# Three chained dense products on 64 graphs beside an eigendecomposition: the hidden product in seven chained products, one masking operation for two, sums of weights over six steps

## What is computed

```python
def _slconv(x, adj, S, W):
    support = jnp.einsum('bnf,fh->bnh', x, W)
    weighting = adj * S
    return jnp.einsum('nm,bmh->bnh', weighting, support)
h = relu(_slconv(h, adj, S, W1))     # 256 -> 512 features: "hid"
h = relu(_slconv(h, adj, S, W2))     # 512 -> 1024
return _slconv(h, adj, S, W3)        # 1024 -> 256
# h at the start is relu(layernorm(x)); the result is added to x
...
# second layer: eigenvectors U of the normalised Laplacian of A = adj
_, U = jnp.linalg.eigh(L_norm)
agg = jnp.einsum('mn,bnd->bmd', U.T, features)
h = relu(agg @ W1 + b1)
out = h @ W2 + b2
return jnp.einsum('nm,bmd->bnd', U, out)
```

## Time and profile before

| what | value |
| --- | --- |
| median of three runs (lowest, highest) | 2261.66 us (2261.61, 2262.51) |
| the profiled execution: own time, span | 2262.78 us, 2261.1 us |
| TensorE busy (modelled ends) | 2238.3 us, 99% |
| VectorE busy | 1932.7 us, 85% |
| ScalarE busy | 1151.1 us, 51% |
| GpSimd busy | 1159.6 us, 51% |
| granted TensorE clock | 1.00 |
| DMA | 90.14 MB, mean 40 GB/s |

### The profile page before, as it was taken

How to read it: one execution, slowest core, us unless ns; L and a number is a source line. 1 busy time by engine, 2 the same in 40 slices (tenths; PEclk the granted TensorE clock), 3 DMA queues, 4 the chain that set the end, 5 groups by cost and what they waited for, 6 DMA issues and landing times.

```text
span 2261.1 us, 47549 instructions
## 1 busy us (share of the span) xinstructions
PE 2238.3 (99%) x12586; PEld 1905.3 (84%) x12586; DVE 1932.7 (85%) x10818; ACT 1151.1 (51%) x2901; POOL 1159.6 (51%) x1889
## 2 busy tenths in 40 slices
PE   8999999999999999999999999999999999999999
PEld 5777888888888888888888888888888888889998
DVE  7999999999888888888777778989999997547776
ACT  5555555555555555555555544444444444344554
POOL 6455555545555555555555557544555554343332
PEclk9999999999999999999999999999999999999999
DMA  3000000000000000000000000000000001024443
GB/s 105 29 29 29 16 24 29 29 29 20 29 29 29 29 29 19 19 28 28 28 28 28 28 29 20 29 29 19 24 25 28 28 28 38 19 80 132 135 132 107
DMA packets 90031, 90.14 MB, mean 40 GB/s; under 512 B 5376, under 2 KB 89088, under 8 KB 89856
## 3 DMA queue, kind: packets, MB, share of 16 engines
q1 hardware_dynamic: 89856, 88.23, 12.2%
HBM read 54.66 MB, written 33.55 MB: 39 GB/s over the span
## 4 chain that ended last, share of the span: by engine, by line
PE 91%; DVE 7%; ACT 1%; issue 1%; POOL 0%; DVEq 0%; ACTq 0%; POOLq 0%
PE ps L1550 74%; PE ps L1740 10%; PE ps L1472 3%; PE ps L1750 1%; DVE A L961 1%; PE ps L1683 1%; DVE A L965 1%; ACT squares L709 1%; DVE prods L998 1%; DVE xrow_sb L970 1%; ACT root_s L711 0%; DVE ps L1013 0%; DVE sc L979 0%; DVE sc L982 0%; DVE qcol L984 0%
## 5 line engine op out<-in xcount | busy, mean ns | idle before, releaser
L501 POOL COPY Eb<-sc 128x1 f32<-128x1 f32 (+1 forms) x254 | 46.7, 184 | 451.6 <-DVE v L986 231.9
L1550 PE MATMUL ps<-agg2T,w 128*128 128x256 f32 x1024 | 239.2, 379 | 0.0
L1550 PE MATMUL ps<-hid2T,xin 128*128 128x256 f32 x1024 | 236.1, 379 | 0.7 <-ACT h2T L754 0.7
L1550 PE MATMUL ps<-weightT,hid 128*128 128x256 f32 x1024 | 236.7, 379 | 0.0
L1550 PE MATMUL ps<-w,aggT 128*128 128x512 f32 x512 | 231.7, 592 | 0.0
L1550 PEld LDWEIGHTS ps<-weightT,hid 128*128 128x128 f32 x1024 | 189.5, 191 | 36.7 <-issue 14.3
L1550 PEld LDWEIGHTS ps<-hid2T,xin 128*128 128x128 f32 x1024 | 189.0, 190 | 26.2 <-ACT h2T L754 1.1
L1550 PEld LDWEIGHTS ps<-agg2T,w 128*128 128x128 f32 x1024 | 188.5, 190 | 25.3
L754 ACT ACTIVATE hid2T<-ps 128x512 f32<-128x512 f32 x256 | 151.0, 590 | 94.9 <-PE ps L1550 92.9
L1166 DVE SCALAR_TENSOR_TENSOR ahead<-ps,ne,ahead 128x14 f32<-128x14 f32 (+1 forms) x1020 | 189.9, 228 | 0.0
L1163 DVE RECIPROCAL ps<-ahead 128x14 f32<-128x14 f32 (+1 forms) x1024 | 188.3, 230 | 0.1
(11 more groups left out here) (387 smaller groups left out, 6194.3 us busy)
## 6 DMA issues: line engine op xcount, KB each, us to landing
xl<-in_x_dram SPq DMA_DIRECT2D x64, 256.0 KB, 2.8
xr<-in_x_dram SPq DMA_DIRECT2D x64, 256.0 KB, 2.8
x_dram<-xr SPq DMA_DIRECT2D x64, 256.0 KB, 2.3
xin<-x_dram SPq DMA_DIRECT2D x64, 256.0 KB, 2.8
out_dram<-xin SPq DMA_DIRECT2D x64, 256.0 KB, 2.2
w<-in_L_gnn_W_dram SPq DMA_DIRECT2D x1, 2048.0 KB, 10.3
w<-in_L_gnn_W_dram SPq DMA_DIRECT2D x1, 1024.0 KB, 12.2
w<-in_L_gnn_W_dram SPq DMA_DIRECT2D x1, 512.0 KB, 5.2
```

The lines of the kernel that those rows point to most:

```text
L501: pool.tensor_copy(Eb[:, bass.ds(k, 1)], sc[:, 4:5])
L1550: ins = pe.matmul(dst, a, b, start=start, stop=stop, skip_group_check=plan_.units[i][0][0] in "PG")
```

## The change

1. **hid.** The four units of `hid` (each two matmuls of 512 columns) become seven, `H1 H5 H6 H2 H7 H3 H4`, each two matmuls of 256 columns. As in P and G, H6 adds onto H1's bank, H3 onto H5's, H7 onto H6's and H4 onto H7's, after the bank was evacuated. GpSimd makes four sums of nodes for each pair (`sum_of_nodes`, into the tile h) and three additions of results (`add_hid`); ScalarE makes seven evacuations and three relus (`finish_hid`) in place of four evacuations. The banks of the units are no longer taken in turn but by the table `bank_of`.
2. **Steps of two blocks.** The two instructions of L1013 become one (`tensor_tensor` with `under`, a copy of the mask in PSUM), and the clearing of L1015 goes; `columns` leaves the head out of the squares instead.
3. **Sums of weights.** Four sums of W1 are made before the first step; those of W2 and W3, made in steps 0 to 3 of pair 0, are made in steps 1 to 5, in another order, and the P units wait for each by itself.
4. `COUNTS_AT`, `REFLECTORS_AT`, `REFINE_AT`, `TURN_AT`, `VECTORS_AT` and `NORMS_AT` are set anew for a pair of 43 units instead of 40.

```diff
         def columns(k0):
 
-            return max(k0, P) if k0 + 1 >= P else k0
+            return max(k0, P) if k0 + 1 >= P else k0 + 1
...
-        COUNTS_AT, REFLECTORS_AT = 34, 3
-        REFINE_AT, TURN_AT, VECTORS_AT = (24, 27, 34, 38, 41, 43, 46), 63, 65
-        NORMS_AT = 22
+        COUNTS_AT, REFLECTORS_AT = 39, 7
+        REFINE_AT, TURN_AT, VECTORS_AT = (38, 41, 48, 50, 53, 55, 59), 75, 77
+        NORMS_AT = 33
...
-            units = [("hid", j, q) for j in range(2) for q in range(NB)]
+            units = [(p, 0, 0) for p in ("H1", "H5", "H6", "H2", "H7", "H3", "H4")]
...
+        BANK_OF = {"H1": 0, "H5": 1, "H6": 0, "H2": 2, "H7": 0, "H3": 1, "H4": 0, "agg": 2, "res": 2}
+        BANK_OF.update({p + n: 0 if n in "1674" else 2 for p in "PG" for n in "1567324"})
+
+        def bank_of(unit):
+            stage, j, q = unit
+            return (3, 2, 0, 1)[2 * q + j] if stage == "agg2" else BANK_OF[stage] + j
...
-        S_TURNS = [(n, half) for half in range(2) for n in (1, 2, 3, 4)]
+        S_TURNS = [(n, half) for n in (1, 2, 4, 3) for half in range(2)]
...
+        HID_ADDS = (("C11", "H1", "H2"), ("C12", "H6", "H3"), ("C22", "H5", "H7"))
...
-        POOL_ORDER = [("turn", n) for n in range(1, 5)] + [("add", n) for n in range(len(ADDS))]
-        POOL_ORDER += [("left", n) for n in range(len(LEFTS))] + [("g3", n) for n in range(len(G3_ADDS))]
+        POOL_ORDER = [("hid", n) for n in range(3)] + [("turn", n) for n in range(1, 5)] + [("add", n) for n in range(len(ADDS))]
+        POOL_ORDER += [("left", n) for n in range(len(LEFTS))] + [("nodes", n) for n in range(1, 5)] + [("g3", n) for n in range(len(G3_ADDS))]
...
+            def sum_of_nodes(pair, n):
+
+                a11, a12, a21, a22 = (aggT[:, j, f, :] for j in range(2) for f in range(2))
+                a, b, op = {1: (a21, a22, ALU.add), 2: (node_block(1), a11, ALU.subtract), 3: (a11, a21, ALU.subtract),
+                            4: (a12, node_block(2), ALU.subtract)}[n]
...
+                pool.tensor_tensor(node_block(n), a, b, op).then_inc(node_sum, 1)
+
+            def add_hid(pair, n):
+
+                name, other, block_ = HID_ADDS[n]
+                pool.wait_ge(evac, before(pair) + FULL.at[block_, 0, 0] + 3)
+                pool.tensor_tensor(hid_block(name), hid_kept(other), hid_block(name), ALU.add).then_inc(hid_added, 1)
...
                     if isinstance(t, int) and t == 0:
                         if s == 0:
+                            pool.wait_ge(evac, 4)
+                            for n in range(1, 5):
+                                sum_of_nodes(0, n)
+                        if s == 1:
                             pool.wait_ge(load_w, 16 * 6)
-                        for n, half in S_TURNS[4 * s:4 * s + 4]:
+                        for n, half in S_TURNS[3 * (s - 1):3 * s] if s else []:
                             sum_of_weights(n, half)
-                        if 2 <= s < 4:
+                        if 4 <= s < 6:
...
+            def finish_hid(pair, n):
+
+                act.wait_ge(hid_added, len(HID_ADDS) * pair + n + 1)
+                block_ = hid_block(HID_ADDS[n][0])
+                act.activation(block_, block_, ACT.Relu).then_inc(hid_fin, 1)
...
+            HID_AFTER = {5: [0], 6: [1], 7: [2]}
...
                 dve.wait_ge(col_ready, k + 2)
-                for b in range(NB):
-                    ins = dve.tensor_scalar(x_next[:, b:b + 1], col[:, b:b + 1], below[:, b, here:here + 1], None, ALU.mult)
-                at(ins)
-                at(dve.memset(head, 0.0), HOUSE - 20)
+                at(dve.tensor_tensor(x_next, col[:, :], under[:, :, here], ALU.mult), HOUSE - 19)
...
-                if stage == "hid":
-                    return group(bank[:, :], [(aggT[:, j, f, P * q:P * q + P], w1[:, f, :]) for f in range(FB)])
+                if stage[0] == "H":
+                    left, right = {"H1": (aggT[:, 0, 0, :], w1_block(0, 0)), "H2": (aggT[:, 0, 1, :], w1_block(1, 0)),
+                                   "H3": (node_block(4), w1_block(1, 1)), "H4": (aggT[:, 1, 1, :], w1sum[:, 3, :]),
+                                   "H5": (node_block(1), w1sum[:, 0, :]), "H6": (node_block(2), w1sum[:, 1, :]),
+                                   "H7": (node_block(3), w1sum[:, 2, :])}[stage]
+                    return [(half[m], left[:, P * m:P * m + P], right, "P" + stage[1] not in ONTO and m == 0, True)
+                            for m in range(NB)]
...
+                if (stage, j, q) == ("agg2", 1, 0):
+                    pe.wait_ge(evac, before(pair) + plan_.at["H4", 0, 0] + 3)
+                elif stage == "agg2":
+                    pe.wait_ge(hid_fin, len(HID_ADDS) * pair + (1, 1, 2, 3)[2 * q + j])
```

More of the change, by code:

```diff
@@ L349, in needs @@
                 return [("add", n)]
+            if kind == "hid":
+                return [("evac", at[HID_ADDS[n][2], 0, 0])]
+            if kind == "hidfin":
+                return [("hid", n)]
+            if kind == "nodes":
+                return [("evac", at["agg", 1, 0])]
             if kind == "turn":
@@ L380, in placed @@
                     if events and all(x in ended for x in needs(*events[0])):
-                        engine = "act" if line in ("evac", "fin") else line
+                        engine = "act" if line in ("evac", "fin", "hidfin") else line
                         start = max([free[engine]] + [ended[x] + 0.1 for x in needs(*events[0])])
-                        ready.append((start, line != "fin", line, engine))
+                        ready.append((start, line not in ("fin", "hidfin"), line, engine))
                 start, _, line, engine = min(ready)
                 kind, n = event = lines[line].pop(0)
-                took = {"unit": size[n] * 62.0 / total if kind == "unit" else 0, "g3": 0.75, "fin": 0.65,
+                took = {"unit": size[n] * 62.0 / total if kind == "unit" else 0, "g3": 0.75, "nodes": 0.75, "fin": 0.65, "hidfin": 0.65,
                         "evac": 0.35 if kind == "evac" and FULL.units[n][0][0] == "G" else 0.65}.get(kind, 1.35)
@@ L410, in placed @@
             return early, late, pool_turns
-        for first, last, steps, _ in GROUPS:
-            assert last - first == 1 or steps % 2 == 0
+        for (first, last, steps, _), k0 in zip(GROUPS, FIRST_STEP):
+            assert last - first == 1 or steps % 2 == 0 and k0 + 1 >= P
         @block.sync
@@ L592, in in_turn @@
                     sum_of_moving(pair, n)
+                elif kind == "hid":
+                    add_hid(pair, n)
+                elif kind == "nodes":
+                    sum_of_nodes(pair + 1, n)
                 elif kind == "add":
@@ L664, in pair_sums @@
             def pair_sums(pair, more, plan_=FULL):
+                for n in range(3):
+                    add_hid(pair, n)
                 for n in range(1, 5):
@@ L672, in pair_sums @@
                         ln_scale(pair + 1, j)
-                for kind, n in POOL_ORDER[4:]:
-                    in_turn(pair, kind, n, plan_)
+                for kind, n in POOL_ORDER[7:]:
+                    if kind != "nodes" or more:
+                        in_turn(pair, kind, n, plan_)
             with pool.Fori(WITH_STEPS, PAIRS - 1) as t:
@@ L753, in evacuate @@
                     act.wait_ge(turn_s, 4 * pair + 4)
-                act.activation(dst, bank, ACT.Relu if stage in ("hid", "P4") else ACT.Copy).then_inc(evac, 1)
+                act.activation(dst, bank, ACT.Relu if stage in ("H4", "P4") else ACT.Copy).then_inc(evac, 1)
             def finish(pair, n):
@@ L846, in pair_body @@
                         finish(pair, n)
+                    for n in HID_AFTER.get(i, []):
+                        finish_hid(pair, n)
                     if more and (stage, j) == ("P2", 1):
@@ L1483, in unit_matmuls @@
                 stage, j, q = plan_.units[i]
-                bank = ring[i % 4]
+                bank = ring[bank_of(plan_.units[i])]
                 half = [bank[:, 0:N], bank[:, N:2 * N]]
```

77 lines of the change are left out of this document (57 added, 20 removed).

## The result

The changed kernel took 2293.28 us (median of 4 runs, 2292.82 to 2293.94), the kernel before beside it 2261.89 (2261.61 to 2262.51): ratio 1.0139, 95% interval 1.0121 to 1.0156. That is 31.4 us slower. The forecast was 12 us slower, with 2284 as the upper end of its range: the sign was right, the size was not.

A forecast was written before the change was run, and what follows sets the result against it. TensorE's own sum was taken to bound most of the kernel, VectorE the start. Terms 5.3 + 4.8 + 2.0 + 0 = +12.1 us on the 2261.1 span, plus 0.6, gave 2273.8 us; range 2265 to 2283, with rivals 2256 to 2284.

The forecast's parts named there:

- Pairs 22 to 31, no steps: Pairs after the reduction: waits of 0.8 us a pair against a gain of 0.84, so no change over ten pairs.
- The last two pairs ... 0: Last two pairs: eigenvector places and a 1.47 us wait for VectorE move; gain may be taken back, counted as 0.
- The weights' sums ... nothing: Early steps: weights' sums of 1.27 us each on GpSimd, at most three a step, used three steps later, cost nothing.
- Rival (c): GpSimd becomes late, step 1's reflector copy passing the next beta and stopping VectorE: 2286 us, chance 0.08.
- a gain of 0.84 for the products: Every pair: hid's matmul passes on TensorE fall from 6.88 to 6.04 us, a gain of 0.84 us.
- the waits of two-block steps: Pairs 5 to 11: TensorE waits 0.33 in step 0, 1.2 in the next; less 0.84, +0.7 us a pair, +4.8 in all.
- Pairs 1 to 3: Pairs where VectorE sets the pace: delays in steps 0 and 1 outweigh VectorE's gain, net +0.5 us a pair.
- the two delays of 0.9 and 1.76: VectorE-paced pairs: q row 0.9 us late in step 0 and 1.76 us late in the next step.
- 1.6 and 0.36: VectorE-paced pairs: 0.18 us saved per step by the single instruction, 1.6 over nine steps and 0.36 over steps 0 and 1.
- Pairs 12 to 20: One-block pairs, forecast as 12 to 21: waits of 0.10 and 1.0, later steps gain 0.86; +0.1 to +0.25 a pair, +2.0.
- 1.6 too little in pair 0: Pair 0: GpSimd's first sums of nodes come behind step 0's reflector copies, delaying TensorE; taken as 3 us in all.
- Rival (a): Throughout the kernel: the forecast waits are absent through unseen slack, 30 us less, 2232 us, chance 0.10.

The follow-up runs named there:

- the run with only the halves moved: Changed kernel with only GpSimd's halves (masks of zeros and ones for the reflector products) moved to pairs 2 to 8: 2289.74 us, ratio 1.0119.

## Why the prediction was wrong in size

The step that failed is the paragraph "Pairs 22 to 31, no steps", with its "nothing is left, 0 x 10". Its working holds for the pairs behind pair 22. Pairs 25 to 28, beside which TensorE does nothing else, took 57.36 us each before and 57.47 after (from the first `weightT,hid` pass to the next pair's), and pairs 23 to 29 together are 0.1 us longer: the three handovers and the relu cost about what the seven products gave. It took pair 22 for one of them. I read the GpSimd rows of a later pair, found 4.61 us of idle time, and never read GpSimd's list at the seam (the place where the steps end and the pairs without steps begin), though the earlier trace rows is itself a view of 1399 to 1401.5 us. The change moved GpSimd's first duty in a pair from behind `agg2` to behind H2, and 17.7 us of other work stood in between. That is 12.3 + 1.8 of the 19 us by which the forecast was short, shown by taking the block away (14.1 by the medians, 13.7 between two passes of the traces).

The same oversight in small is in three other terms. "The last two pairs ... 0" missed that GpSimd's list has the second layer's scalars ahead of pair 31's additions (3.0 us). "The weights' sums ... nothing" missed that those of W3 come between the additions of pair 0 (step 6: 8.52 us for 5.99). And the W1 sums before the first step, which I left out of the sum altogether, held VectorE by 1.9 in the changed kernel's trace. Rival (c) was the right suspect, a late GpSimd, at the wrong place: it looked at reflector copies, which were never late.

What held: a gain of 0.84 for the products (steps 5, 8 and 10 of pair 8 are 0.43, 0.23 and 0.22 shorter), and the waits of two-block steps: of the 1.5 us forecast, step 1 of pair 8 is 1.23 longer and step 0 0.21, and the pair is longer by 0.57 (forecast 0.7). Putting the relu ahead of the root gave back 0.8 of it, so the cause of that wait is shown. Pairs 1 to 3 were 0.3 shorter rather than 0.5 longer. Both halves of that term were off. The run without VectorE's part is 2.0 us a pair above the kernel before there, where the forecast had 2.46 (the two delays of 0.9 and 1.76, less 0.2 for the lighter last steps); and VectorE's part took off 2.3 beside the products, where I had 1.96 (1.6 and 0.36). Pairs 12 to 20 were longer by 0.46 each rather than 0.1 to 0.25. Up to pair 21 the loss was 13.9 us against 12.1 in my terms, and that closeness is in part luck: 3.0 too much in pairs 1 to 4 and 0.8 too much in pairs 5 to 11 hid 1.6 too little in pair 0, 2.2 too little in pairs 12 to 20 and the 1.8 at the start. Rival (a), no waits, is out; with the waits taken away by order and banks the kernel comes to 2237.6, near that rival's 2232.

What stays open is why VectorE's part is worth some 5 us more beside the products, and how far pair 0 could be shortened.

## What to carry to other kernels

When a change gives an engine an earlier duty in a repeated block, read that engine's whole list at every seam where the block's surroundings differ (first pair, last pair, between stages), not at a typical repetition. A product scheme that saves passes pays through handovers: it won here only when the order of the units, the banks and the lists of all three engines were laid out for it. Take a wait away and look one step later before you count the gain.

## What was unexpected of the hardware

After waits of 8.6 and 12.3 us TensorE started at a granted clock of 0.50, and both cost 1.7 to 1.8 us more behind the wait. The clock also differs between executions that run the same instructions: step 0 of pair 0 is the same in the changed kernel and in the run with only the halves moved, and took 8.88 us at 1.00 in the one trace and 10.58 in the other, where the granted clock was 0.50 from 24 to 26 us. So a difference of 1.7 us in pair 0 between two traces says nothing before the clock is compared. VectorE's instructions of 0.16 us took 0.56 to 0.74 us beside GpSimd sums of 0.72 us, in each of the five traces that had the two together.
